# The first query tile's scores over all four row groups of TensorE, in one group of eight

## The reference

```python
x = layernorm(x + attn(x))            # rmsnorm, causal conv, gated delta rule (a scan over 256 steps), Wo, gated MLP
x = layernorm(x + xattn(x, ctx))      # 16 heads of width 16, softmax over 120 context positions
x = layernorm(x + moe(x))             # router, 8 experts, each token to its best one
```

```python
q = (x @ Wq + bq); k = ctx @ Wk + bk; v = ctx @ Wv + bv      # each split in 16 heads of 16
p = softmax(q @ k.T / sqrt(16))                              # per batch and head, 256 x 120
out = (p @ v, heads joined) @ Wo + bo
```

## Time and profile before

| | us |
|---|---|
| median of 3 runs | 1918.45 (1917.17 to 1918.71) |
| the profiled execution | 1916.3 |
| its span, first to last instruction | 1914.1 |
| PE busy in the span | 1373.1 (72%) |
| DVE busy | 1199.6 (63%) |
| POOL busy | 1005.7 (53%) |
| ACT busy | 755.6 (39%) |

### The profile page before, as it was taken

How to read it: one execution, slowest core, us unless ns; L and a number is a source line. 1 busy time by engine, 2 the same in 40 slices (tenths; PEclk the granted TensorE clock), 3 DMA queues, 4 the chain that set the end, 5 groups by cost and what they waited for, 6 DMA issues and landing times. The chain is left out here.

```text
span 1914.1 us, 28138 instructions
## 1 busy us (share of the span) xinstructions
PE 1373.1 (72%) x6660; PEld 942.6 (49%) x6661; DVE 1199.6 (63%) x3351; ACT 755.6 (39%) x2416; POOL 1005.7 (53%) x1246
## 2 busy tenths in 40 slices
PE   6614558500047766678657899996599999999997
PEld 4413446400035555556546677775355555555554
DVE  4499999999799999999772235344232323222222
ACT  5521224401123766667864688886111111111110
POOL 3258998886589998898765323421111111121211
PEclk9857779855568888889968999997799999999999
DMA  4601114600221101110102112323311501501200
GB/s 123 210 25 34 45 34 142 221 37 0 77 67 33 28 26 38 32 32 24 30 17 89 54 39 63 101 70 123 117 42 61 163 22 40 179 30 62 67 17 6
DMA packets 97684, 125.40 MB, mean 66 GB/s; under 512 B 10001, under 2 KB 74952, under 8 KB 95560
## 3 DMA queue, kind: packets, MB, share of 16 engines
q1 hardware_dynamic: 60040, 97.22, 16.1%
q10 hardware_dynamic: 33136, 18.58, 3.3%
q0 software_dynamic: 4432, 8.73, 1.3%
HBM read 89.68 MB, written 35.74 MB: 66 GB/s over the span
## 5 line engine op out<-in xcount | busy, mean ns | idle before, releaser
L238 POOL TENSOR_TENSOR wt<-wt 128x1024 f32<-128x1024 f32 x128 | 301.3, 2354 | 53.0 <-DVE wt L183 32.4
L244 POOL TENSOR_TENSOR wt<-wt 128x512 f32<-128x512 f32 (+2 forms) x384 | 306.6, 799 | 30.1
L1865 PE MATMUL e_ph<-wt,e_g 128*128 x624 | 274.3, 592 | 0.0
L183 DVE SCALAR_TENSOR_TENSOR wt<-wt,scan 128x256 f32<-128x256 f32 x512 | 240.6, 470 | 0.1
L162 DVE TENSOR_REDUCE wt<-wt 128x16 f32<-128x272 f32 x512 | 217.9, 426 | 0.1
L151 DVE TENSOR_TENSOR wt<-wt,scan 128x256 f32<-128x256 f32 x512 | 208.7, 408 | 10.6 <-PEq L261 10.6
L173 DVE TENSOR_TENSOR scan<-wt,scan 128x256 f32<-128x256 f32 x512 | 213.7, 417 | 0.3
L1356 ACT ACTIVATE wt<-p_pX,p_mx 128x120 f32<-128x120 f32 x512 | 176.4, 387 | 75.1 <-DVE p_mx L1143 74.9
L1758 POOL TENSOR_TENSOR e_ve<-e_mv,eps 128x1 f32<-128x1 f32 x39 | 7.4, 189 | 369.1 <-DVE e_mv L1809 369.1
L1488 PE MATMUL p_pm<-p_w_mix,p_oT 128*128 128x256 f32 x128 | 43.5, 498 | 195.5 <-DMA p_oT<-o 165.6
L1865 PEld LDWEIGHTS e_ph<-wt,e_g 128*128 128x128 f32 x624 | 115.5, 190 | 130.8 <-issue 130.8
(11 more groups left out here) (223 smaller groups left out, 2885.5 us busy)
## 6 DMA issues: line engine op xcount, KB each, us to landing
wt<-in_L_ffn_W SPq DMA_DIRECT2D x24, 1024.0 KB, 5.3
qkv<-f_st ACTq DMA_DIRECT2D x48, 256.0 KB, 2.3
p_kE<-kE SPq DMA_DIRECT2D x16, 480.0 KB, 3.7
p_vP<-vP SPq DMA_DIRECT2D x16, 480.0 KB, 4.5
wt<-qkv SPq DMA_DIRECT2D x6, 1024.0 KB, 9.6
e_xt<-routed ACTq DMA_DIRECT2D x39, 130.0 KB, 2.1
f_xt<-in_x SPq DMA_DIRECT2D x16, 256.0 KB, 2.9
p_oT<-o SPq DMA_DIRECT2D x16, 256.0 KB, 2.9
```

The costliest lines, as they stand in the source:

```text
L183: nc.vector.scalar_tensor_tensor(s["S"][:, h, u], s["S"][:, h, (u - 1) % R], s["gate"][:, jb, h, 2, bass.ds(c * R + u, 1)], s["outer"][:], ...
L238: nc.gpsimd.tensor_tensor(x, s["S"][:, h, z * Q:(z + 1) * Q], s["qn"][:, h, z * Q:(z + 1) * Q].rearrange("p t (o d) -> p t o d", o=1).to_b ...
L244: nc.gpsimd.tensor_tensor(x[:, :, :, 0:half], x[:, :, :, 0:half], x[:, :, :, half:2 * half], ALU.add).then_inc(s["o_fold"][h], 1)
L1865: ins = nc.tensor.matmul(ph2[:], g1[:, c // (C1 // 2), c % (C1 // 2)], wt[:, bass.ds(at_b + (W2_AT + c * F2), F2)], start=(c == 0), stop=( ...
```

## The change

`score` keeps only the second tile, x = 2 and 3. The first tile's eight matmuls are issued by a new function `first_scores`, first one for each of the four row groups with g = 0, then one for each with g = 1. The two increments of `score_done` are kept: the first on row group 1's last matmul, the sixth of the eight, the second on row group 3's, the last. All eight stand behind one wait for `PT_out` at d * 8 + 8, where four of them stood behind a wait at d * 8 + 6 before. The new waits' order is `PT_out`, `q_out`, `k_in`.

```diff
--- before.py
+++ after.py
@@ -1516,20 +1516,29 @@
                         ins = nc.tensor.matmul(pq[:, go], wq[:, g, go * P:(go + 1) * P], x1T[:, g], start=(g == 0), stop=(g == G - 1))
                 ins.then_inc(q_done, 1)
 
+            def score_of(q, group, g):
+
+                rows = slice(32 * group, 32 * group + 32)
+                return nc.tensor.matmul(pX[:, group // 2, group % 2, g * 2 * CTX:(g + 1) * 2 * CTX], qT[rows, g, q * P:(q + 1) * P],
+                                        kE[rows, q, g].rearrange("p a c -> p (a c)"), start=True, stop=True)
+
+            def first_scores(c):
+
+                pe.wait_ge(q_out, (c + 1) * G)
+                pe.wait_ge(k_in, c * 16 + 16)
+                for group in range(4):
+                    score_of(0, group, 0)
+                score_of(0, 0, 1)
+                score_of(0, 1, 1).then_inc(score_done, 1)
+                score_of(0, 2, 1)
+                score_of(0, 3, 1).then_inc(score_done, 1)
+
             def score(c, x):
-                q = x // 2
-                if x == 0:
-                    pe.wait_ge(q_out, (c + 1) * G)
-                    pe.wait_ge(k_in, c * 16 + 16)
-                if x >= 2:
-                    pe.wait_ge(exp_done, c * HALVES + (x - 1))
+
+                pe.wait_ge(exp_done, c * HALVES + (x - 1))
                 for g in range(G):
-
                     for i in range(2):
-                        group = x % 2 * 2 + i
-                        rows = slice(32 * group, 32 * group + 32)
-                        ins = nc.tensor.matmul(pX[:, x % 2, i, g * 2 * CTX:(g + 1) * 2 * CTX], qT[rows, g, q * P:(q + 1) * P],
-                                               kE[rows, q, g].rearrange("p a c -> p (a c)"), start=True, stop=True)
+                        ins = score_of(1, x % 2 * 2 + i, g)
                 ins.then_inc(score_done, 1)
 
             def probabilities(d, some):
@@ -1604,11 +1613,8 @@
                     probabilities(d, range(6, 8))
                 if "c" in on:
                     if "d" in on:
-                        pe.wait_ge(PT_out, d * 8 + 6)
-                    score(c, 0)
-                    if "d" in on:
                         pe.wait_ge(PT_out, d * 8 + 8)
-                    score(c, 1)
+                    first_scores(c)
                 if "f" in on:
                     if "c" in on:
                         pe.wait_ge(x1T_out, c + 1)
```

## The result

Device time, median of 20 executions each, taken in turn on one chip:

| | before | after |
|---|---|---|
| median (lowest to highest), us | 1917.49 (1915.57 to 1923.06) | 1921.26 (1917.68 to 1927.85) |
| ratio, with 95% interval | | 1.0024 (1.0016 to 1.0032), + 4.6 us |
| executions above 1923 us | 1 of 20 | 8 of 20 |
| the profiled execution, its span | 1916.3, 1914.1 | 1919.81, 1917.7 |
| PE busy in the span | 1373.1 | 1352.1 |

The account below looks back on a forecast made before the run. It took DVE beside the scan and PE after it as the bounds. Pairs 5 and 6 (1.3), 7 (0.93), 10 to 12 (2.7), 9, 13 and 14 (0.45) and 15 (1.02) sum to + 6.4: 1924.9 us, range 1919.5 to 1929.5.

Parts of the forecast that it names:

- What bounds what: DVE busy beside the scan, PE after it; tile 0's scores wait for ACT's last copy, first maximum 0.93 to 1.02 late.
- The overlap is there already: Pair 8: old order already runs sixteen score records in 1.11 us, so pairs 0 and 8 gain nothing.
- PE's own time, + 0.15: Other fourteen pairs: next work + 0.03 net, plus 0.12 for two further waits, so PE 0.15 us late.
- Loop steps, 2.7: Pairs 10 to 12: maximum 1.02 late, less 0.12 slack before score x = 2, costs 0.90 each, 2.7 us.
- Pairs 1 to 4, 0: DVE is behind; pair 1's scores, ready at + 2.14 against a maximum at + 2.19, are just in time; cost 0.
- Pairs 5 and 6, 1.3: DVE, POOL, ACT, PE chain beside the scan: 0.93 late, 0.28 swallowed by a gap, 0.65 each, 1.3 us.
- Pair 7, 0.93: No down projection in this step; output projection waits for aT behind the Exps; no slack, 0.93 us lost.
- Pair 15, 1.02: Score x = 2 already waits for the first Exps, so the whole delay of 1.02 us is lost.
- Clock: Rival: PE's added idle in loop steps drops the clock to 1.2 GHz, 1935 to 1946 us; chance 0.04.
- the rival of the hidden delay: Pairs 5 to 7 cost nothing and the sequencer adds nothing: 3.3 us later, 1921.8; chance 0.20.
- the sequencer at 0.30: Upper price for PE's two further waits after release, 0.30 us instead of 0.12; sum then some 8 us.
- the rival in which the overlap fails: New order no faster than two groups: sixteen records take 1.91 us, another 0.87 in twelve pairs, 10.4, 1935; chance 0.02.

Follow-up runs that it names:

- the wait alone: Kernel before with only the wait moved: old issue order, x = 0 and x = 1 both behind PT_out + 8; 1922.96 us, ratio 1.0029.
- the fourth: Kernel after with ACT's Exp table loaded ahead of the wait for the maximum, in the loop steps; 1920.91 us, ratio 1.0019.
- the tenth experiment: Kernel before with a small scratch Exp that loads ACT's table early in the loop steps; 1916.69 us, ratio 1.0003.
- the sixth: Kernel after with DVE's small addition (L1171) moved to POOL; 1918.48 us, ratio 1.0009 to the kernel before.
- the eighth: Kernel after plus addition on POOL, early Exp table and, in pairs 9 to 15, one copy on DVE and routing counts behind the last transposes; 1913.45 us, 0.9977.
- the fifth: Kernel before with DVE's small addition (L1171) moved to POOL; 1916.97 us, ratio 0.9998.
- the addition on POOL: DVE's 128 x 2 addition (L1171) moved to POOL in three kernels: before 1916.97 us, new function in pairs 0 to 7 only 1916.46, after 1918.48.
- the third: Kernel before with the new function and its wait in pairs 8 to 15 alone; 1920.81 us, ratio 1.0022.
- that round alone: Kernel before with the new function and its wait in pairs 0 to 7 alone; 1920.38 us, ratio 1.0015.
- the three high executions: Profiled executions of three kernels: only the wait moved (1927.05 us), new function in pairs 0 to 7 alone (1925.17), kernel after with early Exp table (1925.35).

## Why the prediction was right, and where its sizes were off

- **What bounds what.** Right. The sign, the place (the wait for PT_out + 8) and the chain through the Exps were as forecast, and the wait alone reproduces them.
- **The overlap is there already.** Right, and it was the step that decided against a gain: the earlier trace rows showed sixteen records in 1.11 us in pair 8, and the wait alone shows the same in a loop step. The gain was not the order's to give. In pairs 0 and 8 PE's next work starts where it did.
- **PE's own time, + 0.15.** Mis-sized, mildly: + 0.09 in the loop steps, + 0.01 in the written-out ones after the scan. The 0.12 for the two further waits was too much; of the forecast's 0.15 each, pairs 9 and 13 show 0.02 and 0.03 (35.51 to 35.53 and 33.47 to 33.50).
- **Loop steps, 2.7.** Right: 0.87 each, 2.6. The slack of 0.12 before x = 2 and the table load behind the maximum were both read correctly from the earlier trace rows; the fourth and tenth experiments show that mechanism from both sides.
- **Pairs 1 to 4, 0.** In the kernel after DVE waits for no scores there, as forecast. But "just in time" in pair 1 had nothing to spare: in the fourth DVE waits 2.4 us for the scores in pair 1, and in the sixth and the eighth 2.0 in pair 4, where with the old first round it never does. In the sixth this doesn't delay pair 5 (893.9, as in the fifth).
- **Pairs 5 and 6, 1.3.** The chain was right up to POOL: 0.81 late, 0.28 swallowed, + 0.41 in pair 5. But it isn't seen in the end time: with the addition on POOL the new first round costs - 0.4 us, give or take 1.0. Here the term should have been 0.4 to 0.8 with a free end below: a PE that changes its clock in these pairs returns or takes more than it.
- **Pair 7, 0.93.** Not confirmed. The delay is there (first maximum + 0.91), but from T of pair 7 to T of pair 8 all kernels take 91.0 to 92.6 us in no order that follows the change (before 91.32, after 91.54, old first round 90.98 and 91.91, new 91.24 and 91.65). That spread is larger than the term. Not separable.
- **Pair 15, 1.02.** Score x = 2 is 0.91 later; from T to the end of the span it takes 603.2 before and 604.2 after, but 602.6 to 605.1 over the others with either version. Not separable.
- **Clock.** In the loop steps the granted clock stayed at 2.4 GHz throughout, as forecast, and the steps of 36.15, 36.15 and 36.07 are made up of the terms above. Pair 8, which the forecast left unchanged, is 0.7 us longer by a fall of 3.4 us in it; that fall comes without the change too (the fifth) and is missing with it in the third and the fourth.
- **What was missing.** The high group. The terms that the traces confirm add up to about 3: 2.6 in the loop, 0.4 in pair 5. By the medians the two kernels with the addition on POOL are 1.5 apart and the two original ones 3.8; by the ratios it is 2.1 and 4.6. The twelve executions of the kernel after below 1923 us have their median at 1919.2, 1.8 above the kernel before. The difference is the high group, 8 of 20 executions. So the measured loss lay close to + 6.4 partly by luck, through something that the forecast did not name. For the mechanism by itself the rival of the hidden delay, 3.3 us, was the better number.
- **Sums.** Two of the prediction's sums don't come out of its own terms. The range from the hidden delay with 1.8 to the good to the sequencer at 0.30 with 1.8 to the bad is 1920.0 to about 1928.5, not 1919.5 to 1929.5; the measured 1921.3 lies in either. And its list leaves ten pairs without slack (5 to 7 and 9 to 15), not twelve, so the rival in which the overlap fails comes to 8.7 us more, some 1933.6, not 10.4 and 1935.

What stays open: why executions with the new wait fall into the high group more often. It isn't the first round's wait alone: that round alone and the second alone had 3 of 12 each. The new wait moves PE, and with it ACT and POOL, by 0.8 to 1 us against DVE's scan, and it may be that DVE's addition then meets another of POOL's instructions; but the tenth experiment had the full stall without it. Pair 5 took 47.1 us in the three high executions against 44.5 to 45.0 in all others, so a second part of the loss lies there; 1.5 us of it are the attended values shown above, and no run isolated their cause.

## What to carry to other kernels

Before an instruction order is rewritten to use more of TensorE's row groups, look for a step in which the same calls stand without a wait between them: if they overlap there, the order is not what costs, and the wait is. Merging two waits into the later one gives the earlier consumer's slack away, and it shows where a fixed cost, here a table load, follows the first result. When a change of 1 us a step gives several groups of times, look for a short instruction whose length varies by ten times; to learn whether it makes the groups, take it off the engine in both kernels and run all four side by side on one chip, which was missing here.

## What the runs showed of the hardware

- Matmuls of different row groups overlap across calls in program order without being interleaved: sixteen records in 1.11 us with four on two groups and then four on the other two, 1.09 in turn over all four.
- An addition of 128 x 2 float32 values on DVE, mostly 0.13 to 0.18 us, took up to 2.33 us when it started inside a POOL instruction of 128 x 1024, and ended with it.
- ACT's table load of 1.28 us stands behind the wait for the maximum in the hardware loop and ahead of it in the written-out steps; an Exp of 128 x 1 values ahead of the wait moves it.
- Pair 6 with the old first round takes 40.6 or 43.6 us, as its stretch at 1.2 GHz lasts 17.1 or 23.9.
